# A GRU recurrence on Trainium2: the wait for a step's seeds moves from TensorE to VectorE, and the last block's rows are sent in two parts

## What is computed

```python
def reference(x, cond, ...):
    x = x + attention_block(x, cond[:, None, :], ...)   # modulated RMS norm, qkv, 16 heads, softmax, W_out
    def cell(h, x_t):
        gi = x_t @ W_ih + b_ih
        gh = h @ W_hh + b_hh
        i_r, i_z, i_n = split(gi, 3);  h_r, h_z, h_n = split(gh, 3)
        r = sigmoid(i_r + h_r)
        z = sigmoid(i_z + h_z)
        n = tanh(i_n + r * h_n)
        h_new = (1 - z) * n + z * h
        return h_new, h_new
    hs = scan(cell, cond, x over its 512 tokens)
    return x + hs
```

## Time and profile before

| | |
|---|---|
| median of 3 runs | 2147.14 us (2144.82, 2147.14, 2153.47) |
| the profiled execution | 2152.64 us, span 2150.9 us |
| granted TensorE clock over the span | 0.999 |
| TensorE matmul busy | 2117.3 us, 98% |
| VectorE busy | 1311.8 us, 61% |
| ScalarE busy | 1130.8 us, 53% |
| matmuls of the recurrence, line 648 | 49152, 1495.8 us |

### The profile page before, as it was taken

One profiled execution on the slowest core, in us unless ns is written; L12 is line 12 of the kernel. 1 busy time (PEld: TensorE's weight loads), 2 busy tenths in 40 slices (PEclk: granted clock), 3 DMA queues, 4 the chain that ended last, 5 costly groups with the idle time before them and its releaser, 6 DMA issues.

```text
span 2150.9 us, 130641 instructions
## 1 busy us (share of the span) xinstructions
PE 2117.3 (98%) x58001; PEld 1692.1 (79%) x58001; DVE 1311.8 (61%) x5001; ACT 1130.8 (53%) x5055; POOL 188.2 (9%) x227
## 2 busy tenths in 40 slices
PE   8999999999999999999999999999999999999997
PEld 5665666667888888888888888888888888888776
DVE  4766667665556565666666565666566666666555
ACT  5775766665444444445454444454444444444444
POOL 4433333331000000000000000000000000000000
PEclk9999999999999999999999999999999999999999
DMA  6000000004201000001000000000000100000000
GB/s 224 1 21 2 2 21 2 1 1 139 97 21 27 26 20 24 21 22 28 22 25 20 26 22 28 18 25 21 23 23 24 26 22 24 19 26 22 20 9 9
DMA packets 78912, 62.04 MB, mean 29 GB/s; under 512 B 41840, under 2 KB 74124, under 8 KB 78348
## 3 DMA queue, kind: packets, MB, share of 16 engines
q1 hardware_dynamic: 77332, 50.40, 7.9%
q0 software_dynamic: 528, 3.15, 0.4%
q10 hardware_dynamic: 488, 0.15, 0.0%
HBM read 29.80 MB, written 16.78 MB: 22 GB/s over the span
## 4 chain that ended last, share of the span: by engine, by line
PE 95%; DVE 2%; issue 1%; ACT 1%; POOL 1%; DMA 0%; SPq 0%; POOLq 0%; DVEq 0%; ACTq 0%
PE ps L648 64%; PE ps L389 7%; PE ps L545 7%; PE ps L481 7%; PE ps L566 3%; PE ps L582 3%; PE ps L451 2%; PE ps L465 1%; DVE nT L1021 1%; PE ps L456 1%; DVE xb L1032 1%; ACT xb L818 1%; DVE ps L1026 1%; DMA x1T<-in_L_cond_W_emb 0%; POOL qk_rs L362 0%
## 5 line engine op out<-in xcount | busy, mean ns | idle before, releaser
L648 PE MATMUL ps<-wqkv,xb 128*4 128x128 f32 x49152 | 1495.8, 273 | 14.4 <-DVE xb L1032 10.3
L648 PEld LDWEIGHTS ps<-wqkv,xb 128*4 128x4 f32 x49152 | 1231.7, 87 | 247.6 <-DVE xb L1032 200.3
L1021 DVE STREAM_TRANSPOSE rzT<-ps 128x128 f32<-128x128 f32 x512 | 163.1, 318 | 333.1 <-PE ps L648 333.1
L823 ACT ACTIVATE r_pair<-rzT 128x8 f32<-128x8 f32 x512 | 107.8, 210 | 451.8 <-DVE rzT L1021 451.8
L1032 DVE TENSOR_TENSOR_SCAN xb<-z_trip,xb 128x24 f32<-128x24 f32 x1024 | 213.0, 208 | 188.1 <-ACT xb L818 129.8
L818 ACT ACTIVATE xb<-ps 128x16 f32<-128x16 f32 x1024 | 189.8, 185 | 163.5 <-DVE ps L1026 152.7
L481 PE MATMUL ps<-wih,x1T 128*32 128x192 f32 x3392 | 229.4, 326 | 0.1
L780 ACT ACTIVATE probs<-ps,negmax 128x512 f32<-128x512 f32 x256 | 173.2, 689 | 102.6 <-DVE negmax L953 102.5
L830 ACT ACTIVATE z_trip<-znT 128x8 f32<-128x8 f32 x512 | 109.3, 213 | 193.1 <-DVE znT L1021 192.7
L545 PE MATMUL ps<-wqkv,xnT 128*128 128x384 f32 x512 | 204.4, 487 | 1.0 <-ACT xnT L726 1.0
L798 ACT ACTIVATE ps<-seeds 128x256 f32<-128x256 f32 x512 | 194.3, 379 | 0.0
(11 more groups left out here) (87 smaller groups left out, 1375.2 us busy)
## 6 DMA issues: line engine op xcount, KB each, us to landing
gi_spill<-gi_image SPq DMA_DIRECT2D x64, 192.0 KB, 2.2
seeds<-gi_spill SPq DMA_DIRECT2D x226, 32.0 KB
seeds<-gi_spill SPq DMA_DIRECT2D x282, 16.0 KB
seeds<-blank SPq DMA_DIRECT2D x10, 384.0 KB, 3.4
out<-xb SPq DMA_DIRECT2D x240, 16.0 KB
xb<-in_x SPq DMA_DIRECT2D x3, 1024.0 KB, 5.6
wih<-in_L_cond_W_ih SPq DMA_DIRECT2D x1, 3072.0 KB, 16.8
seeds<-blank SPq DMA_DIRECT2D x1, 3072.0 KB, 20.5
```

The source lines that it names most:

```text
L648: last = nc.tensor.matmul(ps[QD * j:QD * j + B, bank, 0:P], hist_flat[:, first:first + 3 * B - 2:3], weights, start=False, stop=False, ski ...
L1021: return nc.vector.transpose(into[:].rearrange("p (r k b s) -> p k r s b", r=4, k=blocks, b=B, s=2), ps[:, bank, first:first + QD * blocks])
```

## The change

In the loop TensorE waits for `seeded` in step 0 only. VectorE now waits for it in every step but the last: in front of the transpose into rzT it waits for the seeds of the following step and then for `rza_sum`. Since VectorE's `h_a` of that step comes behind it, TensorE's next step stays ordered behind its seeds.

The last block's rows are split. VectorE turns the whole block in steps 506 and 507 (`turn_rows`), when its first 24 tokens have been added, and SyncE sends these 24 tokens of each batch by 16 DMAs of `send_rows`, placed in the source in the last four steps. The last eight tokens take the way by TensorE: 16 matmuls with 8 instead of 32 stationary columns (`rows_of_last`), into two PSUM banks instead of one; ScalarE copies the first bank's 256 columns, VectorE the second's, into the area of gi_image, and four DMAs of 16 KB (`send_last`), two on SyncE's and two on ScalarE's queue, send them.

```diff
@@ -118,6 +118,8 @@
         hist = xb_flat[:, D:D + HIST * ENTRY].rearrange("p (t e s) -> p t e s", e=17, s=3)
         hist_flat = xb_flat[:, D:D + HIST * ENTRY]
 
+        last_rows = gi_image[:, 0:2, :].rearrange("p b n -> p (b n)")[:, 0:D]
+
         gate_cols = lambda ap, g, j: ap.rearrange("p (g c j x) -> p g c j x", c=KT, j=4, x=QD)[:, g, :, j, :]
         rzT = sb("rzT", [P, P])
         nT = sb("nT", [P, P // 2])
@@ -168,7 +170,7 @@
         EMB_BANK, VECTORS_BANK = SC[3], SC[2]
         N_COND, N_BEMB, N_GN = B * KT, 2 * KT, KT
 
-        GI_BANKS, ROW_BANK = (6, 7), 7
+        GI_BANKS = (6, 7)
         TURN_STEPS, SEND_STEP, LAST_BLOCK = (3, 5), 7, N_BLK - 1
 
         (ld_cond, ld_emb0, ld_emb1, ld_emb2, ld_emb3, ld_wqkv_first, ld_wqkv_rest, ld_x_first, ld_blank, ld_blank_mid, ld_blank_rest, ld_wout, ld_wih, ld_whh, ld_bias, ld_gi0, ld_gi1, ld_gi2, ld_gi3, ld_x, ld_g, st_gi, st_out) = (
@@ -232,6 +234,10 @@
                                 gi_spill[n % 2, :, rows, 0:2 * P]).then_inc(ld_gi[wave], 16)
                 queue.dma_start(seeds[QD * j + B:QD * j + 2 * B, first:first + count, 2 * P:3 * P],
                                 gi_spill[n % 2, :, rows, 2 * P:3 * P]).then_inc(ld_gi[wave], 16)
+
+        def send_last(queue, b):
+            queue.wait_ge(s["rows_ready"], 2)
+            queue.dma_start(out[b, T - ADD:T, :], last_rows[BLK * b:BLK * b + ADD, :]).then_inc(st_out, 16)
 
         block = ctx.enter_context(nc.Block())
 
@@ -276,9 +282,10 @@
                 sp.dma_start(gi_spill[n % 2, b], gi_image[:, b, :]).then_inc(st_gi, 16)
 
             def send_rows(m, b, i):
+                tokens = BLK if m < LAST_BLOCK else BLK - ADD
                 sp.wait_ge(s["rows_turned"], 2 * (m + 1))
-                sp.dma_start(out[b, m * BLK:m * BLK + BLK, :].rearrange("t (c i x) -> i t c x", c=KT, x=QD)[i],
-                             out_rows[QD * i:QD * i + QD, :].rearrange("t (c b x) -> t b c x", b=B, x=QD)[:, b]).then_inc(st_out, 16)
+                sp.dma_start(out[b, m * BLK:m * BLK + tokens, :].rearrange("t (c i x) -> i t c x", c=KT, x=QD)[i],
+                             out_rows[QD * i:QD * i + tokens, :].rearrange("t (c b x) -> t b c x", b=B, x=QD)[:, b]).then_inc(st_out, 16)
 
             def fill(first, end, landed):
                 sp.dma_start(seeds[:, first:end, :], blank[:].unsqueeze(1).broadcast_to([P, end - first, GCOL])).then_inc(landed, 16)
@@ -325,9 +332,12 @@
                     b, i = divmod(2 * (u - SEND_STEP), 4)
                     send_rows(m - 1, b, i)
                     send_rows(m - 1, b, i + 1)
-            sp.wait_ge(s["rows_ready"], KT)
-            sp.dma_start(out[:, T - BLK:T, :], out_rows).then_inc(st_out, 16)
-            sp.wait_ge(st_out, 16 * 4 * B * LAST_BLOCK + 16)
+                if step >= T - 4:
+                    for i in range(4):
+                        send_rows(LAST_BLOCK, step - (T - 4), i)
+            for b in (0, 1):
+                send_last(sp, b)
+            sp.wait_ge(st_out, 16 * 4 * B * N_BLK + 16 * B)
 
         @block.gpsimd
         def _(pool):
@@ -667,10 +677,10 @@
             pe.wait_ge(s["x1_ready"], FULL_Y + 4)
             open_banks((3,)).then_inc(s["banks_open"], 1)
 
-            def rows_of_block(m, c):
+            def rows_of_last(c):
                 for b in range(B):
-                    last = nc.tensor.matmul(ps[BLK * b:BLK * b + BLK, ROW_BANK, P * c:P * c + P],
-                                            x1T[:, c, b, BLK * m:BLK * m + BLK], ident[:], start=True, stop=True,
+                    last = nc.tensor.matmul(ps[BLK * b:BLK * b + ADD, GI_BANKS[c // 2], P * c:P * c + P],
+                                            x1T[:, c, b, T - ADD:T], ident[:], start=True, stop=True,
                                             tile_position=(0, BLK * b))
                 return last
 
@@ -678,7 +688,8 @@
                 m, u = divmod(step, BLK)
                 rza_bank, rbna_bank, znb_bank = step_banks(step)
                 pe.wait_ge(s["h_a"], step + 1)
-                pe.wait_ge(s["seeded"], step + 1)
+                if step == 0:
+                    pe.wait_ge(s["seeded"], 1)
                 hidden_side(rza_bank, RZ_A, step, 0)
                 hidden_side(rbna_bank, RB_NA, step, 0)
                 pe.wait_ge(s["h_b"], step + 1)
@@ -696,9 +707,12 @@
                     else:
                         gi_eighth(n, b, i, GI_BANKS[b % 2])
 
+            pe.wait_ge(s["gi_evac"], B * N_BLK)
             pe.wait_ge(s["out_added"], T // ADD)
             for c in range(KT):
-                rows_of_block(N_BLK - 1, c).then_inc(s["rows_ps"], 1)
+                last = rows_of_last(c)
+                if c % 2 == 1:
+                    last.then_inc(s["rows_ps"], 1)
 
         @block.scalar
         def _(act):
@@ -798,10 +812,6 @@
                 nc.scalar.activation(ps[:, rza_bank:znb_bank + 1:2, 0:P].rearrange("p h (s n) -> p h s n", s=2),
                                      sixths[:, :, 0:3:2, :], ACT.Copy).then_inc(s["seeded"], 1)
 
-            def copy_rows(c):
-                nc.scalar.activation(out_rows[:, P * c:P * c + P], ps[:, ROW_BANK, P * c:P * c + P],
-                                     ACT.Copy).then_inc(s["rows_ready"], 1)
-
             act.wait_ge(st_gi, 16 * B)
             act.wait_ge(ld_blank, 16)
             for j in (2, 3):
@@ -835,10 +845,11 @@
                         wave = (step + 2) // WAVE % 4
                         act.wait_ge(ld_gi[wave], gi_landed((step + 2) // BLK, wave))
                     seed(step + 2)
-            act.wait_ge(st_out, 16 * 4 * B * LAST_BLOCK)
-            for c in range(KT):
-                act.wait_ge(s["rows_ps"], KT)
-                copy_rows(c)
+            act.wait_ge(st_gi, 16 * B * N_BLK)
+            act.wait_ge(s["rows_ps"], 1)
+            nc.scalar.activation(last_rows[:, 0:2 * P], ps[:, GI_BANKS[0], 0:2 * P], ACT.Copy).then_inc(s["rows_ready"], 1)
+            for b in (2, 3):
+                send_last(act, b)
 
         @block.vector
         def _(dve):
@@ -1007,7 +1018,7 @@
                 last.then_inc(s["out_added"], 1)
 
             def turn_rows(m, pair):
-                dve.wait_ge(s["out_added"], BLK // ADD * (m + 1))
+                dve.wait_ge(s["out_added"], BLK // ADD * (m + 1) - (m == LAST_BLOCK))
                 if m > 0 and pair == 0:
                     dve.wait_ge(st_out, 16 * 4 * B * m)
                 nc.vector.transpose(out_rows[:, 2 * P * pair:2 * P * pair + 2 * P].rearrange("p (c b x) -> p c b x", c=2, x=QD),
@@ -1033,6 +1044,8 @@
                         next_elements(step, half), z_trip[:].rearrange("p e s -> p (e s)")[:, 24 * half:24 * half + 24],
                         elements(step, half), 0.0, ALU.mult, ALU.add)
 
+                if step + 1 < T:
+                    dve.wait_ge(s["seeded"], step + 2)
                 dve.wait_ge(s["rza_sum"], step + 1)
                 transpose_sums(rzT, rza_bank, 0, 4).then_inc(s["rzaT_ready"], 1)
 
@@ -1064,9 +1077,14 @@
                     add_out(step - 1 - ADD)
                 if m > 0 and u in TURN_STEPS:
                     turn_rows(m - 1, TURN_STEPS.index(u))
+                if step in (T - 6, T - 5):
+                    turn_rows(LAST_BLOCK, step - (T - 6))
             dve.wait_ge(s["h_a"], T + 1)
             dve.wait_ge(s["h_b"], T + 1)
             add_out(T - ADD)
+            dve.wait_ge(st_gi, 16 * B * N_BLK)
+            dve.wait_ge(s["rows_ps"], 2)
+            nc.vector.tensor_copy(last_rows[:, 2 * P:4 * P], ps[:, GI_BANKS[1], 2 * P:4 * P]).then_inc(s["rows_ready"], 1)
 
 
 # ---- launch: one core; inputs and outputs as the reference has them ----
```

## The result

Median of 16 runs 2138.4 us (2136.0 to 2145.5); the kernel before 2146.7 us (16 runs, 2141.8 to 2157.2). The ratio is 0.9958, 95% interval 0.9945 to 0.9971: 8.3 us faster by the medians, 6 to 12 by the interval. The forecast of 2148.4 us, range 2142 to 2157, is missed on the fast side. That a change of less than 0.5% had been called likely did come true, but for another reason than the one given. The profiled execution took 2137.8 us, with a span of 2135.5.

The account below looks back on a forecast made before the run. The prediction took a 3.06 us chain of latencies per step, not TensorE's rate, to bound the kernel. Terms 0 + 5.1 + 0 - 3.8 = +1.3 us on 2147.1 gave 2148.4 us, range 2142 to 2157.

Parts of the forecast that it names:

- Part 1: TensorE's loop: dropping its 51 ns wait for seeded each step gains 0, with 0.05 us a step as far bound.
- there is nothing to gain: TensorE's loop: the wait ran 1.0 us ahead of h_a and the load started 0.05 us behind release, so 0.
- The rival that TensorE was held up by its extra wait: TensorE's loop: 51 ns a step, 26 us, would go; -25 us with the other terms, 2122; chance 0.05.
- Part 2: VectorE before rzT: separate wait for rza_sum delays it 0.07 us, 0.06 hidden, 0.01 a step exposed, 5.1 us in all.
- from there on it is a chain of small operations: Each step from nT's transpose at 2136.90: nT, scan, tanh, new state, h_a at 2137.85, all on the loop.
- only the second 32 are on the loop: TensorE's 64 matmuls counted in one piece: 32 behind h_a, 32 behind h_b; only those behind h_b set the pace.
- 1.17 + 0.95 + 0.94: One step's loop: h_b to nT's transpose, then to h_a, then the second half; 3.06 us of latencies.
- 511 x 0.01 = 5.1 us: Loop cost of rzT's delay on VectorE after the cover behind the sigmoid; bounds 0 to 10 us.
- Part 3: Steps 506 and 507 and SyncE's 16 earlier sends: cost 0; sends take 12.2 us, done by 2142.3, before the last sends.
- Part 4: End of the kernel behind the last h_b: split rows and four smaller sends give back 3.8 us, bounds 2.0 and 4.5.
- The sum: Whole kernel: 0 + 5.1 + 0 - 3.8 = +1.3 us, so 2148.4 us against the median.
- the two terms that were known to be uncertain: Range's stated sources: step term (2143.3 to 2153.5 with the end's 3.8) and the runs' median, perhaps 3 us elsewhere.

Follow-up runs that it names:

- e1: Changed kernel with TensorE's per-step wait for seeded put back and VectorE's removed, so only the new end remains; ratio 0.9983 to the kernel before.
- e3: Changed kernel with the per-step wait for seeded on TensorE as well as on VectorE; 2145.6 us, ratio 0.9985 to the kernel before.
- e2: Kernel before with only the wait for seeded moved from TensorE to VectorE, old end kept; 2141.4 us, ratio 0.9960 to the kernel before.
- s2: Changed kernel with four idle TensorE semaphore increments ahead of h_a in every fourth step, 512 in all; ratio 1.0001 to the kernel before.
- e10: Changed kernel with one small 8-column matmul a step on TensorE ahead of the wait for h_b; ratio 1.0013 to the kernel before.

## Why the prediction was wrong, point by point

**Part 1, the wait leaves TensorE: wrong, the step that failed.** The term was 0, since the wait's instruction ran 1.0 us ahead of h_a (0.75 in the median step) and the load behind h_a started 0.05 us behind its release. The load behind h_a starts as soon behind its release in the new trace as in the old one. The step that failed is from "the wait is early" to "there is nothing to gain": 511 instructions more also pass through TensorE's instruction supply. In e1 and e3, where the instruction stays, there are 80 and 68 stalls; in e2, where it goes, 36. The term measured -8 us by e2's medians, with an interval of -5 to -12 (-4.4 by the first pair of medians less the end's 3.9, -13.7 by the two profiled executions). The rival that TensorE was held up by its extra wait had the right sign, but 26 us and the wrong place: it put 51 ns on each step, where a quiet step pays nothing and some 30 to 70 borders more do. A hint stood in the profile: the earlier trace rows show a quiet step of 3.07, and 512 of 3.067 make 1570 us, while the loop took 1606. I never asked where those 36 us went, though the weights' loads had 63 waits of the kind "issue". The first step has 11.8 of them, in both kernels; 18.2 are in the steps with stalls. That taking one instruction out would lower them could not be read there.

**Part 2, the wait comes to VectorE: sizes right, place wrong.** The separate wait cost 0.070 us, the cover behind the sigmoid shrank from 0.16 to 0.10, and 0.012 us came out at the first scan: all as worked out. What failed here is "from there on it is a chain of small operations" and "only the second 32 are on the loop". All 64 matmuls behind h_b are, up to znb_sum, and the first scan has some 0.036 us of cover. That 1.17 + 0.95 + 0.94 still gave the right 3.06 is no support for it: the last term is the time from h_a to h_b on the clock, not a chain that begins at h_a. So 511 x 0.01 = 5.1 us became 0.

**Part 3, the earlier sends: 0, right.** The step stayed at 3.066 us while they went out. Their size was off: 13.4 us for 12.2, 0.84 each, so that 0.9 us of margin are left where 1.9 were expected.

**Part 4, the end: right.** 3.93 us against 3.8. Its terms, as forecast and as measured: add_out to TensorE's start, from the last state's end, 0.68 and 0.71; matmuls 1.12 and 1.10; to the copy 0.10 and 0.09; copy 0.42 and 0.42; second send 0.3 and 0.3; landing 2.2 and about 2.0 (2133.44 + 1.6 against an issue at 2132.78 + 0.3); behind the landing 0.4 and 0.4. The rule of the Trainium skill (DMA: Bandwidth & Descriptors, Rules for kernel authors) that under 64 KB one pays mostly overhead did not turn against the change: four sends of eight rows on two queues landed sooner than the one of 256 KB, whose wait had been 5.3 us. Size, shape and queues changed together, so no run here shows which of them did it.

**The sum.** -8 for +0 and 0 for +5.1 is 13 us against a forecast of +1.3 in e2's and e1's measure, and 10 us in the first pair of medians: 2138.4 for 2148.4. The range's lower end was made of the two terms that were known to be uncertain; a term that rested on "it is early, so it is free" had been given no width.

**What stays open.** Why one instruction more in a step makes fetches late. With 208 instructions a step the borders of 256 fall on the same 13 places of 16 steps (16 x 208 = 13 x 256), and with 209 they drift; but s2, whose borders move in jumps, and e10, with 212 a step, cost as much, and in before the stalls stood at all places of the step. The number of extra instructions does not set the price either: one a step and four a step cost about the same, and a second wait cost more than the first. In the kernels with the extra instruction the fetch also begins later behind the previous border (median 1.06 us in before, 0.84 in after). None of this is shown to be the cause. That the pauses are late fetches is read from the traces' packets; no run took the fetches themselves away.

## What to carry to other kernels

Compare the loop's time with the number of steps times the median step before costing an edit: what is left over is where an edit can act that leaves the quiet step alone. On an engine with a long unrolled loop, an instruction that ran early and hidden was not free; here the wait cost nothing measurable on VectorE, with 13 instructions in most steps, and 8 us on TensorE, with 208. Of two waits of an operation write the late one first. Find the loop by asking, at every hand-over, which event the waiting engine started right behind (znT 24 ns behind znb_sum), and follow that one; operations in sequence on the clock need not be a chain.

## What the runs showed of the hardware

TensorE's instructions came in packets of 16 KB, 256 instructions (456 packets with 7.47 MB; the stalls stand 256 instructions apart), and late ones stopped it for 0.1 to 1.1 us with no releaser in the profile. One satisfied wait or one increment more in each step, on top of 208, went with 65 to 94 such stalls instead of 19 to 44, and with 8 to 12 us more against the kernel without it beside it; so did a small matmul, which is four instructions. A second satisfied wait a step cost 17.8 us more. Where the steps had 192 instructions and the DMA queues moved 27 packets a us instead of 42, almost no border stalled (0 to 2 of some 39 in each run). The first-written of two waits stayed with its operation (24 ns behind its event), and the other came 94 ns behind.
